# Attention scores, decay and product with v: from 128x128 tiles over two sequences to 64x64 blocks per sequence, in a fused layer on one Trainium2 core

## The chip, the cores and the metric

The kernel runs on one core of a Trainium2 chip. The metric is device time in microseconds of one execution, as a median of repeated runs. The core's engines run side by side and meet only at semaphores: TensorE (PE in the profile; its weight loads are the separate row PEld), VectorE (DVE), ScalarE (ACT), GpSimd (POOL), and SyncE (SP), whose queue issues the DMAs. SBUF and PSUM have 128 partitions. TensorE reads SBUF and writes PSUM, which has eight banks of 128 x 512 float32 here.

## What is computed

x holds 64 sequences of 64 tokens with 512 features. The first half is a gated linear attention with a per-head decay, the second a LoRA-adapted dense layer followed by a ternary feed-forward layer. Cut to what matters:

```python
def _L0_attn_ref(hidden_states, Wq, Wk, Wv, Wb, bb, Wg, Wo, ...):   # H = 16, DK = DV = 128
    q = hidden_states @ Wq; k = hidden_states @ Wk; v = hidden_states @ Wv
    beta = jax.nn.sigmoid(hidden_states @ Wb + bb)
    gate = silu(hidden_states @ Wg)
    q = layernorm(silu(causal_dwconv(q, qconv_w, qconv_b)), qn_w, qn_b)   # per head
    k = layernorm(silu(causal_dwconv(k, kconv_w, kconv_b)), kn_w, kn_b)
    def step(S, inp):
        q_t, k_t, v_t, b_t = inp
        b = b_t[..., None, None]
        S = (1.0 - b) * S + b * (v_t[..., :, None] * k_t[..., None, :])
        o_t = jnp.einsum('bhvk,bhk->bhv', S, q_t)
        return (S, o_t)
    _, os = lax.scan(step, S0, (qs, ks_, vs, bs))
    return (o * gate) @ Wo
x = x + _L0_attn_ref(_L0_cond_ref(x, itok_B_0_7, L0_cond_weights), ...)
x = x + _L0_ffn_ref(_L0_cond2_ref(x, ...), L0_ffn_weight, L0_ffn_bias)
```

The kernel doesn't run the recurrence over tokens. For one head it forms the scores k^T q of every pair of tokens, multiplies them by the decay (the product of 1 - beta between the two tokens, zero where the key comes later or is of another sequence), and multiplies the result with beta * v.

## The kernel before

The 4096 tokens are taken in four groups of 1024. In a group the 16 heads are taken in four sets of four (Fori loop over s), so there are 16 such sets in a run. A set has eight units, n = 0 to 7: a head (n // 2) with one half of the group's tokens (n % 2), which is 512 tokens or eight sequences of 64.

Each engine has its own instruction stream, written out by hand in the loop over n; semaphores tie the streams. On TensorE, iteration n issues: project q(n) (12 float32r matmuls of 512 columns, helper `three`, L959), variance(n-1) (L1031, L1032), project k(n), score(n-2) (L1093), project g(n), attend(n-2) (L1103), centre q and k (L1081, L1082). In iterations 0 and 1 there is no score or attend; the product for v (`values`) is there instead. After iteration 7 comes a tail: output projections (`project_out`, in pieces) with score and attend of units 6 and 7 between them.

The lines around the change:
- score(n), L1093: four matmuls, each of 128 tokens (two sequences) against the same 128, into the bank m0. The trace has two records and two weight loads for each of them.
- scan(n), L703, on VectorE: `tensor_tensor_scan` makes the decay of all 512 columns from `keep` (a row of 1 - beta with zero at each sequence's first token, broadcast to 128 partitions by the DMA at L329) and `ident4`, four identity matrices side by side. Half of each 128x128 tile that results is zero, since it belongs to two different sequences.
- weigh(n), L687, VectorE: decay = m0 * decay, 128 x 512.
- attend(n), L1103: four matmuls of a 128x128 tile of v with the 128x128 tile of decay, into the bank m1.
- gate_out(n), L695 and L697, VectorE: gt = m1 * gt, then a rounded copy to og_hi. POOL makes og_lo from both (L505).
- affine(n), L493, POOL: the last step of the layer norm of q and k, which score(n) waits for.

VectorE's order in iteration n is: three convolution taps of q(n) (L663), scan(n-2), three taps of k(n), weigh(n-2), silu_lo of q and k (L669), newton(n-1) (L644), normalise(n-1) (L653), gate_out(n-2). POOL's is: affine(n-2), scale_centred(n-1) (L486), silu_hi (L499), square_lo(n) (L511), gated_lo(n-2) (L505). In the first group POOL also splits the weights (L450, L452) between these.

score(n) waits for affine(n) and for weigh(n-1), which reads m0. attend(n) waits for weigh(n) and for gate_out(n-1), which reads m1. SP loads `keep` for unit n after scan(n-2) has been done, into one of two halves of the tile, as soon as the waits for weight loads ahead of it in its queue are over.

## Time and profile before

| | us |
|---|---|
| median of 3 runs | 2904.72 |
| lowest, highest | 2903.71, 2907.93 |
| profiled execution, first to last instruction | 2907.7 |

The profiled execution's span is thus 3 us above the median of the runs. In the profile a group of instructions is named by its line, engine, operation and the tiles that it writes and reads; "m" stands for m0 and m1, "gen" for the two variance banks, "r_q", "r_k" and "r_odd" for the normalised q and k of even and odd units. Where a row has a bracket, the engine was idle for that long just before, and the name behind the arrow is what ended the wait ("issue": nothing that the profile shows). Starts and lengths are in us unless marked ns.

### The profile page before, as it was taken

How to read it: one execution, taken by the hardware profiler on the slowest of the kernel's cores; microseconds unless marked ns; L12 is line 12 of the kernel's file. 1: busy time of each engine (PE TensorE's matmuls, PEld its weight loads, DVE VectorE, ACT ScalarE, POOL GpSimd, SP SyncE). 2: the span in 40 equal slices, each digit the busy share in tenths (PEclk: the TensorE clock that was granted, in tenths of full speed). 3: DMA queues.
4: the chain of work that ended last, by engine and by line, in shares of the span. 5: the costliest groups of instructions: out<-in, count | busy, mean ns of one | idle time of the engine just before them, and what ended most of it. 6: DMA issues, size and time to landing. Idle time of an engine off the chain costs nothing.

```text
span 2907.7 us, 40276 instructions
## 1 busy us (share of the span) xinstructions
PE 2585.2 (89%) x12124; PEld 2057.5 (71%) x12136; DVE 1960.1 (67%) x2773; ACT 1561.9 (54%) x2393; POOL 1675.2 (58%) x1450
## 2 busy tenths in 40 slices
PE   4789898898898989999889898989898899998988
PEld 4667676676676777777667776767677677776766
DVE  4484857667658485767666758584865857667685
ACT  2463746456157374746436557483724747565562
POOL 2695968769427374645635637273752646556474
PEclk9999999999999999999999999999999999999999
DMA  6533333333342222222323122222223313222321
GB/s 153 165 117 105 115 108 98 105 98 107 102 135 76 66 90 76 94 65 90 96 94 113 62 97 71 88 83 73 83 94 115 92 63 97 76 83 61 108 88 43
DMA packets 155807, 272.12 MB, mean 94 GB/s; under 512 B 29786, under 2 KB 55898, under 8 KB 155738
## 3 DMA queue, kind: packets, MB, share of 16 engines
q1 hardware_dynamic: 155738, 271.26, 30.0%
q8 instruction: 37, 0.61, 0.1%
q14 instruction: 32, 0.26, 0.0%
HBM read 215.37 MB, written 55.84 MB: 93 GB/s over the span
## 4 chain that ended last, share of the span: by engine, by line
PE 72%; DVE 11%; issue 9%; POOL 4%; ACT 3%; SPq 1%; DMA 0%; POOLq 0%; DVEq 0%; ACTq 0%
PE pj_q L959 22%; PE pj_k L959 14%; PE m L959 10%; PE cen_q L959 4%; PE m L1093 3%; PE m L1103 3%; PE gen L959 3%; PE cen_k L959 3%; PE gen L1031 2%; DVE y_k L663 2%; DVE decay L703 2%; PE gen L1032 2%; DVE acc L710 2%; PE cen_k L1081 1%; POOL og_lo L505 1%
## 5 line engine op out<-in xcount | busy, mean ns | idle before, releaser
L663 DVE SCALAR_TENSOR_TENSOR y_q<-pj_q,conv,y_q 128x504 f32<-128x504 f32 (+2 forms) x384 | 281.5, 733 | 183.3 <-ACT y_q L867 173.4
L959 PE MATMUL pj_k<-ht_hi,wk 128*128 128x512 f32 x1024 | 348.4, 402 | 23.6 <-POOL wk L452 23.6
L511 POOL TENSOR_TENSOR sq_lo_q<-y_q,sq_hi_q 128x512 fp32r<-128x512 f32 x128 | 188.1, 1470 | 304.9 <-ACT y_q L880 304.9
L663 DVE SCALAR_TENSOR_TENSOR y_k<-pj_k,conv,y_k 128x504 f32<-128x504 f32 (+2 forms) x384 | 281.2, 732 | 119.4 <-ACT y_k L867 110.3
L959 PE MATMUL pj_q<-ht_hi,wq 128*128 128x512 f32 x1024 | 343.5, 396 | 12.8 <-DVE acc L710 9.4
L959 PE MATMUL pj_q<-ht_hi,wg 128*128 128x512 f32 x1024 | 346.6, 399 | 1.1 <-POOL wg L452 1.1
L505 POOL TENSOR_TENSOR og_lo<-gt,og_hi 128x512 fp32r<-128x512 f32 x128 | 178.3, 1393 | 149.6 <-DVE og_hi L697 149.6
L959 PEld LDWEIGHTS pj_k<-ht_hi,wk 128*128 128x128 f32 x1024 | 197.8, 193 | 71.7 <-POOL wk L452 27.1
L959 PEld LDWEIGHTS pj_q<-ht_hi,wq 128*128 128x128 f32 x1024 | 194.3, 190 | 64.5 <-DVE acc L710 14.4
L959 PE MATMUL m<-wv,ht_hi 128*128 128x512 f32 x768 | 236.8, 389 | 0.0
L499 POOL TENSOR_SCALAR s_hi_q<-y_q 128x512 fp32r<-128x512 f32 x128 | 79.2, 619 | 259.2 <-ACT y_q L872 259.2
L959 PEld LDWEIGHTS pj_q<-ht_hi,wg 128*128 128x128 f32 x1024 | 192.6, 188 | 40.3 <-issue 1.4
L511 POOL TENSOR_TENSOR sq_lo_k<-y_k,sq_hi_k 128x512 fp32r<-128x512 f32 x128 | 205.2, 1603 | 0.2 <-ACT y_k L880 0.2
L959 PE MATMUL pj_k<-ht_lo,wk 128*128 128x512 f32 x512 | 205.0, 400 | 0.0
L867 ACT ACT_TABLE_LOAD x16 | 20.5, 1283 | 337.9 <-PE pj_q L959 333.4
L959 PE MATMUL pj_q<-ht_lo,wq 128*128 128x512 f32 x512 | 201.0, 393 | 0.0
L959 PE MATMUL pj_q<-ht_lo,wg 128*128 128x512 f32 x512 | 199.8, 390 | 0.0
L679 DVE TENSOR_TENSOR v<-m,beta_tok 128x512 f32<-128x512 f32 x96 | 66.2, 690 | 193.3 <-PE m L959 193.3
L703 DVE TENSOR_TENSOR_SCAN decay<-keep,ident 128x512 f32<-128x512 f32 x128 | 187.2, 1463 | 0.0
L1103 PEld LDWEIGHTS m<-decay,v 128*128 128x128 f32 x1024 | 135.2, 196 | 53.4 <-DVE decay L687 45.5
L1103 PE MATMUL m<-decay,v 128*128 128x128 f32 x1024 | 141.8, 283 | 33.9 <-DVE decay L687 33.4
L959 PEld LDWEIGHTS m<-wv,ht_hi 128*128 128x128 f32 x768 | 144.2, 188 | 30.7
(309 smaller groups left out, 6938.2 us busy)
## 6 DMA issues: line engine op xcount, KB each, us to landing
keep<-keep_rows SPq DMA_DIRECT2D x128, 256.0 KB, 3.4
wo<-parts SPq DMA_DIRECT2D x48, 512.0 KB, 5.9
wq<-parts SPq DMA_DIRECT2D x48, 512.0 KB, 3.6
wk<-parts SPq DMA_DIRECT2D x48, 512.0 KB, 3.6
wg<-parts SPq DMA_DIRECT2D x48, 512.0 KB, 3.6
wv<-parts SPq DMA_DIRECT2D x48, 512.0 KB, 5.8
parts<-wv SPq DMA_DIRECT2D x20, 512.0 KB, 3.4
parts<-wq SPq DMA_DIRECT2D x17, 512.0 KB, 3.0
```

The source lines that it names most:

```text
L499: nc.gpsimd.tensor_scalar(s_hi[x_][:], y[x_][:], 1.0, 0.0, ALU.mult, ALU.add).then_inc(S[f"shi_{x_}"], 1)
L505: nc.gpsimd.tensor_tensor(og_lo[:, n // 2, cols], gt[n % 3][:], og_hi[:, n // 2, cols].bitcast(F32), ALU.subtract).then_inc(S["oglo_done"], 1)
L511: nc.gpsimd.tensor_tensor(sq_lo[x_][:], y[x_][:], sq_hi[x_][:].bitcast(F32), ALU.subtract).then_inc(S[f"sqlo_{x_}"], 1)
L663: V.scalar_tensor_tensor(out=yy[:, :, k:], in0=pp[:, :, :L - k], scalar=conv[:, i, j, 3 - k:4 - k], in1=yy[:, :, k:], op0=ALU.mult, op1=AL ...
L679: V.tensor_tensor(v[:, i, :].rearrange("p (h c) -> p h c", h=SET), v_banks[i][:].rearrange("p (h c) -> p h c", h=SET), bt, ALU.mult).then_ ...
L703: V.tensor_tensor_scan(decay[:], keep[:, n % 2, :], ident4[:].rearrange("p a b -> p (a b)"), 0.0, ALU.mult, ALU.add).then_inc(S["scanned"], 1)
L710: V.tensor_tensor(acc[:, i, :], acc[:, i, :], wo_banks[i % 4][:], ALU.add).then_inc(S["acc_done"], 1)
L959: last = T.matmul(psum, a, b, start=start and n == 0 and m == 0, stop=stop and n == len(pairs) - 1 and m == 2)
L1031: T.matmul(var[x_][:], mean[:], sq_hi[x_][:], start=True, stop=False)
L1032: T.matmul(var[x_][:], mean[:], sq_lo[x_][:], start=False, stop=True).then_inc(S[f"var_{x_}"], 1)
L1093: mm = T.matmul(m0[:, cols], r["k"][n % 2][:, cols], r["q"][n % 2][:, cols], start=True, stop=True)
L1103: mm = T.matmul(m1[:, cols], v[:, HT * (n % 2) + i, (n // 2) * P:(n // 2 + 1) * P], decay[:, cols], start=True, stop=True)
```

## The change

The scores of one sequence need only 64 x 64 values. The change keeps, for a unit, the four even sequences on partitions 0 to 63 and the four odd ones on partitions 64 to 127, each in 256 columns.

- score(n): eight matmuls with 64 columns of weights and 64 moving columns, contraction over 128 partitions. The result of an even sequence goes to partitions 0 to 63 of m0, of an odd one to partitions 64 to 127, at column 64 * (b // 2).
- keep, scan, weigh: all 128 partitions but 256 columns. `keep` is loaded with two DMAs for a unit (one for each half of the partitions), each of 64 partitions x 4 runs of 64 values; the even half has the even sequences' rows. `ident_in` takes the place of `ident4`.
- attend(n): eight matmuls with contraction over 64 partitions (0 to 63 or 64 to 127), 128 columns of weights (v) and 64 moving columns. Even sequences write m1, odd ones m0, 256 columns each.
- gate_out(n): two multiplications of 128 x 256 (m1 for the even, m0 for the odd sequences, with the even or odd 64-column pieces of gt), and the same copy of 512 columns.
- Waits: score(n) now waits for gate_out(n-1) in place of weigh(n-1), as m0 holds a part of attend's result. values(2), which writes m0, waits for the previous set's gate_out.
- Setup: eight copies of 64x64 in place of four of 128x128.

```diff
-        keep = sb("keep", [P, 2, HALF])
+        keep = sb("keep", [P, 2, HPAIRS])
...
-                        sp.dma_start(keep[:, n % 2, :], row.broadcast_to([P, HALF])).then_inc(S[f"keep_in{n % 2}"], 16)
+                        rows = row.rearrange("o (i b t) -> o b i t", b=2, t=L)
+                        for b in range(2):
+                            sp.dma_start(keep[b * L:(b + 1) * L, n % 2, :].rearrange("p (i t) -> p i t", t=L),
+                                         rows[:, b].broadcast_to([L, HT, L])).then_inc(S[f"keep_in{n % 2}"], 16)
...
-                        V.tensor_tensor(decay[:], m0[:], decay[:], ALU.mult).then_inc(S["weighed"], 1)
+                        V.tensor_tensor(decay[:, 0:HPAIRS], m0[:, 0:HPAIRS], decay[:, 0:HPAIRS], ALU.mult
+                                        ).then_inc(S["weighed"], 1)
...
-                        V.tensor_tensor(t[:], m1[:], t[:], ALU.mult).then_inc(S["og_done"], 1)
-                        dve.wait_ge(S["og_done"], of_set("og_done", g, s, UNITS, n + 1))
+                        for b, bank_ in enumerate((m1, m0)):
+                            th = t[:].rearrange("p (i b t) -> p b i t", b=2, t=L)[:, b]
+                            V.tensor_tensor(th, bank_[:, 0:HPAIRS].rearrange("p (i t) -> p i t", t=L), th, ALU.mult
+                                            ).then_inc(S["og_done"], 1)
+                        dve.wait_ge(S["og_done"], of_set("og_done", g, s, 2 * UNITS, 2 * n + 2))
...
-                        V.tensor_tensor_scan(decay[:], keep[:, n % 2, :], ident4[:].rearrange("p a b -> p (a b)"),
+                        V.tensor_tensor_scan(decay[:, 0:HPAIRS], keep[:, n % 2, :], ident_in[:].rearrange("p a b -> p (a b)"),
...
-                        pe.wait_ge(S["weighed"], of_set("weighed", g, s, UNITS, n))
+                        pe.wait_ge(S["og_done"], of_set("og_done", g, s, 2 * UNITS, 2 * n))
...
-                        for i in range(HT):
-                            cols = slice(i * P, (i + 1) * P)
-                            mm = T.matmul(m0[:, cols], r["k"][n % 2][:, cols], r["q"][n % 2][:, cols], start=True, stop=True)
+                        for b in range(HROWS):
+                            cols, at = slice(b * L, (b + 1) * L), L * (b % 2)
+                            mm = T.matmul(m0[at:at + L, b // 2 * L:(b // 2 + 1) * L], r["k"][n % 2][:, cols],
+                                          r["q"][n % 2][:, cols], start=True, stop=True)
...
-                        pe.wait_ge(S["og_done"], of_set("og_done", g, s, UNITS, n))
...
-                        for i in range(HT):
-                            cols = slice(i * P, (i + 1) * P)
-                            mm = T.matmul(m1[:, cols], v[:, HT * (n % 2) + i, (n // 2) * P:(n // 2 + 1) * P],
-                                          decay[:, cols], start=True, stop=True)
+                        for b in range(HROWS):
+                            at, cols = L * (b % 2), slice(b // 2 * L, (b // 2 + 1) * L)
+                            mm = T.matmul((m1, m0)[b % 2][:, cols],
+                                          v[at:at + L, HT * (n % 2) + b // 2, (n // 2) * P:(n // 2 + 1) * P],
+                                          decay[at:at + L, cols], start=True, stop=True)
```

TensorE's stream at the score of an odd unit, before (m is m0 here; each row is an instruction of the program, x3 three more like it):

```order
L959 MATMUL pj_k<-ht_hi,wk 128x512
L1093 MATMUL m<-r_odd 128x128 [waits weighed,aff_k,aff_q]
L1093 MATMUL m<-r_odd 128x128 x3
L1054 REGISTER_ALU
L959 MATMUL pj_q<-ht_hi,wg 128x512 [waits tap_q]
```

and in the changed kernel:

```order
L969 MATMUL pj_k<-ht_hi,wk 128x512
L1098 REGISTER_ALU [waits aff_k,aff_q]
L1103 MATMUL m<-r_odd 64x64 [waits og_done]
L1103 MATMUL m<-r_odd 64x64 x7
L1064 REGISTER_ALU
L969 MATMUL pj_q<-ht_hi,wg 128x512 [waits tap_q]
```

The score stands at the same place between project k and project g; it is eight matmuls in place of four, and waits for og_done in place of weighed. VectorE's stream at gate_out, before:

```order
L653 SCALAR_TENSOR_TENSOR r_odd<-t_k,c_k 128x512 [waits rc_k,t2_k]
L695 TENSOR_TENSOR gt<-m,gt 128x512 [waits gated,pv]
L697 CAST og_hi<-gt 128x512 [waits og_done]
L663 SCALAR_TENSOR_TENSOR y_q<-pj_q,conv,y_q 128x8x63 [waits tap0_q]
L662 REGISTER_ALU
```

and in the changed kernel:

```order
L659 SCALAR_TENSOR_TENSOR r_odd<-t_k,c_k 128x512 [waits rc_k,t2_k]
L704 TENSOR_TENSOR gt<-m,gt 128x4x64 [waits gated,pv]
L704 TENSOR_TENSOR gt<-m,gt 128x4x64
L706 ISA
L707 CAST og_hi<-gt 128x512 [waits og_done]
L669 SCALAR_TENSOR_TENSOR y_q<-pj_q,conv,y_q 128x8x63 [waits tap0_q]
```

One more multiplication stands ahead of the copy; the rest of the stream keeps its order.

## Rows read from the trace of the kernel before

**Rows 1.** The page: busy time of each engine, and the chain's shares.
```profile
PE 2585.2 (89%) x12124; PEld 2057.5 (71%) x12136; DVE 1960.1 (67%) x2773; ACT 1561.9 (54%) x2393; POOL 1675.2 (58%) x1450
...
PE 72%; DVE 11%; issue 9%; POOL 4%; ACT 3%; SPq 1%; DMA 0%; POOLq 0%; DVEq 0%; ACTq 0%
```

**Rows 2.** Timeline of one middle iteration: start, length, engine, line, operation, tiles, count.
```profile
1062.28 0.68 DVE L695 TENSOR_TENSOR gt<-m,gt 128x512 f32<-128x512 f32 x1
...
1063.58 0.47 PE L1031 MATMUL gen<-sq_hi_k,mean 128*128 128x512 f32 x1 [0.94 <-issue]
...
1063.85 1.29 POOL L505 TENSOR_TENSOR og_lo<-gt,og_hi 128x512 fp32r<-128x512 f32 x1 [0.36 <-DVE og_hi L697]
...
1065.13 0.77 POOL L493 TENSOR_SCALAR r_odd<-r_odd,ln_q 128x512 f32<-128x512 f32 x1
...
1065.87 1.26 DVE L703 TENSOR_TENSOR_SCAN decay<-keep,ident 128x512 f32<-128x512 f32 x1
1065.88 1.74 POOL L493 TENSOR_SCALAR r_odd<-r_odd,ln_k 128x512 f32<-128x512 f32 x1
...
1067.73 1.13 PE L1093 MATMUL m<-r_odd 128*128 128x128 f32 x8 [0.68 <-issue]
...
1068.61 0.48 PE L959 MATMUL pj_q<-ht_hi,wg 128*128 128x512 f32 x1
...
1068.93 0.39 PE L959 MATMUL pj_q<-ht_lo,wg 128*128 128x512 f32 x1
...
1071.45 1.05 PE L1103 MATMUL m<-decay,v 128*128 128x128 f32 x8
...
1072.26 0.48 PE L1081 MATMUL cen_q<-s_hi_q,center 128*128 128x512 f32 x1
...
1072.80 0.69 DVE L644 SCALAR_TENSOR_TENSOR t_q<-gen,t_q 128x512 f32<-128x512 f32 x1 [0.15 <-ACT t_q L858]
...
1081.77 1.13 PE L1093 MATMUL m<-r_q,r_k 128*128 128x128 f32 x8 [0.67 <-issue]
```

**Rows 3.** Timeline, the same set's iterations 2 and 3.
```profile
1023.27 2.31 DVE L703 TENSOR_TENSOR_SCAN decay<-keep,ident 128x512 f32<-128x512 f32 x1
...
1028.40 1.82 PE L1103 MATMUL m<-decay,v 128*128 128x128 f32 x8 [1.86 <-DVE decay L687]
...
1037.86 2.36 DVE L703 TENSOR_TENSOR_SCAN decay<-keep,ident 128x512 f32<-128x512 f32 x1
```

**Rows 4.** Waits of the whole run: total us, times, longest us.
```profile
PE m L1103 <- DVE decay L687: 33.4, 21, 1.9
```

**Rows 5.** Timeline, the same set's tail.
```profile
1113.59 1.22 DVE L703 TENSOR_TENSOR_SCAN decay<-keep,ident 128x512 f32<-128x512 f32 x1
...
1113.76 2.11 POOL L505 TENSOR_TENSOR og_lo<-gt,og_hi 128x512 fp32r<-128x512 f32 x1 [1.72 <-DVE og_hi L697]
...
1115.92 0.74 PE L959 MATMUL cen_q<-wo,og_hi 128*128 128x512 f32 x2 [1.39 <-POOL og_lo L505]
```

**Rows 6.** Groups by line and shape: busy us, mean ns of one, idle before.
```profile
L703 DVE TENSOR_TENSOR_SCAN decay<-keep,ident 128x512 f32<-128x512 f32 x128 | 187.2, 1463 | 0.0
...
L663 DVE SCALAR_TENSOR_TENSOR y_q<-pj_q,conv,y_q 128x504 f32<-128x504 f32 x128 | 94.6, 739 | 174.1 <-ACT y_q L867 173.4
...
L663 DVE SCALAR_TENSOR_TENSOR y_q<-pj_q,conv,y_q 128x488 f32<-128x488 f32 x128 | 93.0, 726 | 4.6
...
L695 DVE TENSOR_TENSOR gt<-m,gt 128x512 f32<-128x512 f32 x128 | 87.2, 682 | 105.4 <-PE m L1103 105.4
```

**Rows 7.** The shortest float32 matmuls of the trace, as a group (columns as rows 6).
```profile
L1019 PE MATMUL m<-ident,y_k 16*128 16x16 f32 x16 | 1.6, 206 | 2.1 <-ACT y_k L842 2.1
```

**Rows 8.** Timeline, four of these matmuls in a row.
```profile
60.30 0.39 PE L1019 MATMUL m<-ident,y_k 16*128 16x16 f32 x4 [0.51 <-ACT y_k L842]
```

**Rows 9.** Timeline of SP's queue: the load of keep for unit 7.
```profile
1100.61 0.33 SPq L329 DMA_DIRECT2D keep<-keep_rows  x1
```

**Rows 10.** The page's DMA issues: count, KB each, us from issue to landing.
```profile
keep<-keep_rows SPq DMA_DIRECT2D x128, 256.0 KB, 3.4
```

More of the change, by code:

```diff
@@ L50, in adaln_attn_ffn @@
     PAIRS = TILES // 2
+    HPAIRS = HALF // 2
     SMALL = 10
@@ L91, in adaln_attn_ffn @@
         ident_bf = sb("ident_bf", [P, P], BF16)
-        ident4 = sb("ident4", [P, HT, P])
+        ident_in = sb("ident_in", [P, HT, L])
         center = sb("center", [P, P], F32R)
@@ L135, in adaln_attn_ffn @@
         SETUP_LOADS = 1 + KC + 4 + 4 + 1 + 2
-        SETUP_DVE = 33
+        SETUP_DVE = 37
         pj = {"q": bank("pj_q"), "k": bank("pj_k")}
@@ L580, in _ @@
             for t in range(HT):
-                step(V.tensor_copy(ident4[:, t, :], ident[:]))
+                for b in range(2):
+                    half = slice(b * L, (b + 1) * L)
+                    step(V.tensor_copy(ident_in[half, t, :], ident[half, half]))
             dve.wait_ge(S["wb_in"], 16)
@@ L694, in gate_out @@
                         dve.wait_ge(S["gated"], of_set("gated", g, s, UNITS, n + 1))
-                        V.tensor_tensor(t[:], m1[:], t[:], ALU.mult).then_inc(S["og_done"], 1)
-                        dve.wait_ge(S["og_done"], of_set("og_done", g, s, UNITS, n + 1))
+                        for b, bank_ in enumerate((m1, m0)):
[3 more added lines that the diff above has]
+                        dve.wait_ge(S["og_done"], of_set("og_done", g, s, 2 * UNITS, 2 * n + 2))
                         V.tensor_copy(hi, t[:]).then_inc(S["oghi_done"], 1)
                     def scan(n):
-                        dve.wait_ge(S[f"keep_in{n % 2}"], of_set(f"keep_in{n % 2}", g, s, UNITS // 2 * 16, 16 * (n // 2 + 1)))
+                        dve.wait_ge(S[f"keep_in{n % 2}"], of_set(f"keep_in{n % 2}", g, s, UNITS // 2 * 32, 32 * (n // 2 + 1)))
                         dve.wait_ge(S["pv"], of_set("pv", g, s, UNITS, n))
-                        V.tensor_tensor_scan(decay[:], keep[:, n % 2, :], ident4[:].rearrange("p a b -> p (a b)"),
+                        V.tensor_tensor_scan(decay[:, 0:HPAIRS], keep[:, n % 2, :], ident_in[:].rearrange("p a b -> p (a b)"),
                                              0.0, ALU.mult, ALU.add).then_inc(S["scanned"], 1)
@@ L965, in _ @@
             pe.wait_ge(S["setup_in"], 16 * SETUP_LOADS)
-            pe.wait_ge(S["setup_dve"], 7)
+            pe.wait_ge(S["setup_dve"], 11)
             for k in range(KC):
@@ L980, in _ @@
             mm.then_inc(S["setup_pe"], 1)
-            pe.wait_ge(S["setup_dve"], 29)
+            pe.wait_ge(S["setup_dve"], 33)
             for t in range(KC):
@@ L1065, in values @@
                             pe.wait_ge(S["beta_tok_done"], of_group("beta_tok_done", g, 1, 1))
-                            pe.wait_ge(S["weighed"], of_set("weighed", g, s, UNITS, 0))
+                            pe.wait_ge(S["og_done"], of_set("og_done", g, s, 2 * UNITS, 0))
                         elif i == 3:
-                            pe.wait_ge(S["og_done"], of_set("og_done", g, s, UNITS, 0))
+                            pe.wait_ge(S["og_done"], of_set("og_done", g, s, 2 * UNITS, 0))
                         else:
```

## Prediction

> **What bounds the kernel now.** I read the page's busy times and its chain first, then the timeline of a middle iteration, of the start of a set and of its tail, then the waits, the groups by shape, and the DMA lines.
>
> TensorE is busy for 89% of the span and carries 72% of the chain, with 9% of "issue" in it [rows 1]. That reads like a TensorE bound with small gaps; the gaps are what to look at. In a middle iteration TensorE stops twice: 0.94 us before the variance of k, and 0.68 us before the score [rows 2]. The second has no releaser in the profile, but POOL's affine of k runs from 1065.88 for 1.74 us and so ends at 1067.62, 0.11 us before the score's start at 1067.73: the score waits for POOL. From one score to the next it is 1081.77 - 1067.73 = 14.04 us. The loop that closes in this time is: score, project g, ACT's squares of r, VectorE's newton (which waits only 0.15 us, for ACT), normalise and gate_out, POOL's og_lo (which waits 0.36 us for VectorE), affine of q, affine of k, and again the score. TensorE has 0.94 + 0.68 = 1.6 us of slack in it, VectorE and POOL next to none.
>
> Two more places stop TensorE. In iteration 2 of the set the first attend waits 1.86 us for weigh [rows 3]; over the run this wait stands 21 times with 33.4 us, the longest 1.9 [rows 4]: once in each of the 16 sets (16 x 1.86 = 29.8) and a few shorter ones in iteration 3. Behind it is VectorE, whose scan takes 2.31 us there and 2.36 in iteration 3 [rows 3] against 1.26 in a middle iteration [rows 2]. And in the tail an output projection waits 1.39 us for og_lo [rows 5].
>
> **The change, part by part.** Sums are made against the profiled execution, 2907.7 us, which stands 3 us above the median of the runs.
>
> *The scan*, half as many columns. Its mean is 1463 ns, and the shortest kind 1.22 us [rows 5, 6]. By columns it halves to about 0.65, with a fixed part that stays to 0.75 or so. What counts is where it stands. In a middle iteration it has idle time behind it, but it runs beside POOL's affine of k, and that takes 1.74 us where the affine of q just before takes 0.77 [rows 2]. The excess of 0.97 us comes with a scan of 1.26 at the same start; the tail shows it again (og_lo of 2.11 us beside a scan of 1.22, against 1.29 elsewhere, an excess of 0.82) [rows 2, 5]. I take the excess to shrink with the scan: -0.45 us (between 0, if it isn't the scan's doing, and -0.6). In iterations 2 and 3 the scan lies on VectorE's path to weigh: 2.31 halves to 1.15.
>
> *weigh*, half the columns. *gate_out*, two halves in place of one whole. A 512-column product from PSUM takes 682 ns [rows 6]. The half-size one lies between 341 ns (all by column) and 474: three taps of other widths give a slope, 739 - 726 = 13 ns for 16 columns, 0.81 ns a column, so 682 - 256 x 0.81 = 474 [rows 6]. I take 0.42. weigh then gains 0.26, and gate_out costs 2 x 0.42 - 0.68 = +0.16 us (0 to 0.27). gate_out is on the closing loop: og_lo waits for it.
>
> *Middle iterations (n = 4 to 7), VectorE and POOL alone*: -0.45 + 0.16 = -0.3 us on the loop above. A second loop (variance, project k, taps, silu, silu_lo, newton) is only 0.15 us behind it by VectorE's wait [rows 2] and gains nothing but part of weigh. I take -0.25 an iteration, 4 x -0.25 = -1.0 us a set.
>
> *Iterations 2 and 3*: weigh(0) comes 1.15 + 0.26 = 1.4 us earlier; the 1.86 us wait covers that fully, so -1.4. In iteration 3 the scan again gives up to 1.2, but the taps of k can't start before TensorE's project k and ACT's first tap, so only half of it counts: -0.6. Together -2.0 us a set.
>
> *Tail*: og_lo -0.4, gate_out +0.16: -0.25 us a set.
>
> VectorE and POOL together give -(1.0 + 2.0 + 0.25) = -3.25 us a set, x 16 = -52 us.
>
> *Score and attend on TensorE*: this is the unknown. Now eight records of 128 columns take 0.88 us from the score to project g (1067.73 to 1068.61) and 0.81 from attend to centre (1071.45 to 1072.26) [rows 2], 0.11 and 0.10 a record. The change makes sixteen of each, with half the moving columns. The trace has no record of 64 columns. The nearest are the transposes with 16 moving columns and 128 columns of weights: four take 0.39 us with the last's own 0.206, so (0.39 - 0.206) / 3 = 0.061 us a record [rows 7, 8]. That is the price if a record with few columns is bound by its weight load and issue. Upper end: 0.11 a record as now, because the weights of attend are still 128 columns wide: 16 x 0.11 = 1.76, +0.9 us. Lower end: the two halves of the array work at once and a pair costs what one record of half the columns costs: 16 x 0.028 = 0.44, -0.45 us. I take 0.061, the row it is nearest to in size: 16 x 0.061 = 0.98, so +0.10 for the score and +0.17 for attend.
>
> *Change of shape in the array*: after the score the first matmul of project g takes 0.32 us to the next (1068.61 to 1068.93), where such matmuls follow at 0.23 [rows 2]. A switch back thus costs 0.09 already. Going from a whole array to halves may add the same once more around each of the two: +0.1 for the pair (0 to 0.4).
>
> The Trainium skill ("TensorEngine Tiling (Array Packing)", Key Properties) says that a change of the tiling mode drains TensorE, and that distinct tiles load weights and multiply in parallel. No row here shows a switch between tilings of the kind the change brings; the first sentence would put the cost of the switches to the upper end, the second that of the records to the lower.
>
> So a unit costs TensorE 0.10 + 0.17 + 0.1 = +0.37 us. Of that the two units in the tail count whole, as TensorE runs there without other slack. The six before them lie partly under waits (TensorE's 1.6 us of slack in the middle, 0.46 left of the 1.86 at the start), but the score itself is on the closing loop: I count half. 2 + 6 / 2 = 5 units a set: 5 x 0.37 = 1.85 us, x 16 = +30 us.
>
> *Costs of nothing.* The score's new wait for gate_out(n-1): it starts at 1062.28 and would end by 1063.2, the score comes at 1067.73 [rows 2]; 4.5 us of cover, and project g and all behind it would queue if that were gone. The wait of values(2) has longer cover (two projections and a v product lie between). The keep loads: twice the DMAs, runs of 256 bytes, half the bytes. The latest of a set is issued at 1100.61 and used by the scan at 1113.59 [rows 5, 9]; 13 us of cover for something that lands in 3.4 [rows 10]. Behind it on SP's queue stand only the next set's loads. Setup: four more small copies that TensorE's first transposes wait for, under 1 us in all.
>
> **Sum**: 2907.7 - 52 + 30 = 2885.7 in the profiled execution, 2883 as a median.
>
> **The rivals.**
>
> *A. Records near 0.06 us, as above.* Between a pair cost of +0.15 and +0.6 us a unit: -52 + 80 x 0.15 = -40 to -52 + 48 = -4 us, so 2865 to 2901. Chance 0.45.
>
> *B. The weight loads rule (slower).* The place is attend: its weights are as wide as before and there are twice as many, so sixteen records at 0.11. With the score at 0.061 and the switches: 0.10 + 0.9 + 0.1 = +1.1 us a unit, x 80 = +88, less 52 = +36: 2941. If the score's records too stay at 0.11 (a load that can't run beside the matmul before it): +1.9 a unit, +100 us, 3005. It decides for slower at 52 / 80 = 0.65 us a unit. For it: nothing in the trace shows two weight loads at once. Against it: the 16-column row has the same 128 columns of weights and comes at 0.061. The Trainium skill ("TensorE: Matmul & The Clock Gate", The mechanism) says that a weight load overlaps a matmul in flight only when the row group differs. The score's halves share their rows, and by that its loads would stand bare, as in the second form of this rival; attend's would be hidden. Chance 0.30, of which 0.06 for both.
>
> *C. The halves run at once.* -0.3 to -0.45 us for each of score and attend, against +0.1 for switches: -0.6 us a unit. Where TensorE isn't the bound that gives less: the tail's 2 units whole, of the six others a third: 4 x -0.6 x 16 = -38, with -52: -90, so 2815. Between A and C (-60) lies 2845. For it: the two halves have their own partitions in and out. Chance 0.20.
>
> *D. The excess on POOL's affine isn't the scan's*, and with gate_out longer the middle doesn't gain: +0.1 an iteration in place of -0.25, 4 x 0.35 x 16 = +22 on A: 2905, no change. Chance 0.05.
>
> **How the numbers follow.** The forecast is A's middle, 2883. The range takes in C down to 2830 and the first form of B up to 2950, and leaves out the last part of C and the second form of B, with the tails of the others about 0.2. A measurement here can tell 0.2%, 5.8 us. Faster: A but for its last part (0.40), all of C (0.20), some of D (0.01) make 0.61. Same: A's end, part of B's low end and D, 0.09. Slower: 0.30.
>
> **What would show it.** Right: the score's wait in a middle iteration below 0.5 us, POOL's affine of k near 1.3, scans of 0.7, the first attend's wait of 1.86 down to about 0.5, sixteen score records within 1.0 us, middle iterations of about 13.9 us. Wrong: attend of 1.7 us or more from its start to the centring (B), of 0.6 or less (C), an affine of k still at 1.7 beside a scan of 0.7 (D), or keep landing after the scan asks for it.

## The result, and the profile after

The changed kernel takes 2879.9 us (median; 2878.1 to 2887.6), the kernel before 2904.8. The ratio is 0.9916, with a 95% interval of 0.9902 to 0.993: faster by 0.8%. The profiled execution spans 2876.0 us against 2907.7, so there are 31.7 us to account for.

The page of the kernel after, busy times, the DMA queue that carries instructions, and the chain's shares (as [rows 1]):

```profile
PE 2600.1 (90%) x14172; PEld 2007.4 (70%) x14184; DVE 1863.6 (65%) x2905; ACT 1571.0 (55%) x2393; POOL 1604.2 (56%) x1450
...
q8 instruction: 149, 2.44, 0.3%
...
PE 59%; POOL 13%; issue 13%; DVE 10%; ACT 4%; SPq 1%; DMA 0%; POOLq 0%; DVEq 0%; ACTq 0%
```

VectorE lost 97 us of work and POOL, whose work was not touched, 71 us. TensorE has 2048 more matmul records (two for each of 1024 more matmuls of the program), and the chain, 72% TensorE before, now lies 59% on it.

Timeline of a middle iteration after (start, length, engine, line, operation, tiles, count; as [rows 2]). L704 is gate_out, L509 og_lo, L497 the affine, L713 the scan, L1103 score, L1113 attend:

```profile
1063.19 0.74 DVE L704 TENSOR_TENSOR gt<-m,gt 128x256 f32<-128x256 f32 x2
...
1066.05 0.78 POOL L497 TENSOR_SCALAR r_odd<-r_odd,ln_q 128x512 f32<-128x512 f32 x1
1066.79 0.70 DVE L713 TENSOR_TENSOR_SCAN decay<-keep,ident_in 128x256 f32<-128x256 f32 x1
1066.81 1.25 POOL L497 TENSOR_SCALAR r_odd<-r_odd,ln_k 128x512 f32<-128x512 f32 x1
...
1068.30 0.69 PE L1103 MATMUL m<-r_odd 128*64 128x64 f32 x16 [0.33 <-POOL r_odd L497]
1068.92 0.50 PE L969 MATMUL pj_q<-ht_hi,wg 128*128 128x512 f32 x1
...
1071.86 1.11 PE L1113 MATMUL m<-decay,v 64*128 64x64 f32 x16
1072.90 0.50 PE L1091 MATMUL cen_q<-s_hi_q,center 128*128 128x512 f32 x1
...
1082.02 0.69 PE L1103 MATMUL m<-r_q,r_k 128*64 128x64 f32 x16 [0.37 <-POOL r_k L497]
```

The scan went from 1.26 to 0.70 us, and POOL's affine of k beside it from 1.74 to 1.25. The score waits 0.33 us in place of 0.68 and comes every 13.72 us (1082.02 - 1068.30) in place of 14.04. The score's sixteen records last 0.62 us to the next matmul, where eight took 0.88; attend's take 1.04 where eight took 0.81.

The start of a set and its tail (as [rows 3] and [rows 5]): the first attend's wait is 1.14 us for 1.86, and og_lo takes 1.60 us for 2.11.

```profile
1026.21 1.77 DVE L713 TENSOR_TENSOR_SCAN decay<-keep,ident_in 128x256 f32<-128x256 f32 x1
1030.53 1.11 PE L1113 MATMUL m<-decay,v 64*128 64x64 f32 x16 [1.14 <-DVE decay L693]
...
1113.65 1.60 POOL L509 TENSOR_TENSOR og_lo<-gt,og_hi 128x512 fp32r<-128x512 f32 x1 [2.25 <-DVE og_hi L707]
...
1115.30 0.73 PE L969 MATMUL cen_q<-wo,og_hi 128*128 128x512 f32 x2 [0.73 <-POOL og_lo L509]
```

**The gain isn't even.** The starts of the attends cut the span into pieces. I use two: the mean time from one set to the next in group 3 (in these two kernels groups 1 and 2 give the same within 0.3), and the time from the first attend of group 0 to the first of group 1. Group 0 has four sets as well, but POOL also splits the weights there.

| us | before | after | difference |
|---|---|---|---|
| start to first attend | 128.89 | 126.54 | -2.4 |
| group 0, to group 1's first attend | 742.9 | 750.2 | +7.3 |
| from there to the end (12 sets) | 2035.9 | 1999.3 | -36.6 |
| one set in group 3 | 156.74 | 153.87 | -2.9 |

Groups 1 to 3 gained twice what I forecast (1.4 us a set), and group 0 lost. The two misses nearly cancel. The experiments ask for the cause of each.

### The profile page after: what moved, and what is told of

It is laid out like the page before. It is cut to its first block, busy times and chain, and to the rows that moved or that the text cites. A ratio compares the mean times of both kernels' runs of the same rounds, so it can differ in the third digit from the quotient of the medians.

```text
span 2876.0 us, 45128 instructions
## 1 busy us (share of the span) xinstructions
PE 2600.1 (90%) x14172; PEld 2007.4 (70%) x14184; DVE 1863.6 (65%) x2905; ACT 1571.0 (55%) x2393; POOL 1604.2 (56%) x1450
## 3 DMA queue, kind: packets, MB, share of 16 engines
q8 instruction: 149, 2.44, 0.3%
## 4 chain that ended last, share of the span: by engine, by line
PE 59%; POOL 13%; issue 13%; DVE 10%; ACT 4%; SPq 1%; DMA 0%; POOLq 0%; DVEq 0%; ACTq 0%
PE pj_q L969 17%; PE m L969 10%; PE pj_k L969 9%; PE cen_q L969 5%; POOL sq_lo_k L515 4%; PE m L1113 3%; PE gen L969 3%; DVE y_k L669 3%; PE cen_k L969 3%; POOL r_odd L497 2%; PE m L1103 2%; POOL sq_lo_q L515 2%; DVE acc L720 1%; ACT y_q L890 1%; POOL og_lo L509 1%
## 5 line engine op out<-in xcount | busy, mean ns | idle before, releaser
L515 POOL TENSOR_TENSOR sq_lo_q<-y_q,sq_hi_q 128x512 fp32r<-128x512 f32 x128 | 191.7, 1498 | 279.5 <-ACT y_q L890 279.5
L509 POOL TENSOR_TENSOR og_lo<-gt,og_hi 128x512 fp32r<-128x512 f32 x128 | 170.1, 1329 | 174.3 <-DVE og_hi L707 174.3
L515 POOL TENSOR_TENSOR sq_lo_k<-y_k,sq_hi_k 128x512 fp32r<-128x512 f32 x128 | 206.7, 1615 | 0.3 <-ACT y_k L890 0.3
L704 DVE TENSOR_TENSOR gt<-m,gt 128x256 f32<-128x256 f32 x256 | 95.3, 411 | 124.9 <-PE m L1113 124.9
L1113 PEld LDWEIGHTS m<-decay,v 64*128 64x128 f32 x2048 | 124.2, 187 | 64.6 <-DVE decay L693 37.1
```

Of the source, the lines that this page charges most:

```text
L509: nc.gpsimd.tensor_tensor(og_lo[:, n // 2, cols], gt[n % 3][:], og_hi[:, n // 2, cols].bitcast(F32), ALU.subtract).then_inc(S["oglo_done"], 1)
L515: nc.gpsimd.tensor_tensor(sq_lo[x_][:], y[x_][:], sq_hi[x_][:].bitcast(F32), ALU.subtract).then_inc(S[f"sqlo_{x_}"], 1)
L704: V.tensor_tensor(th, bank_[:, 0:HPAIRS].rearrange("p (i t) -> p i t", t=L), th, ALU.mult).then_inc(S["og_done"], 1)
L1113: mm = T.matmul((m1, m0)[b % 2][:, cols], v[at:at + L, HT * (n % 2) + b // 2, (n // 2) * P:(n // 2 + 1) * P], decay[at:at + L, cols], star ...
```

## Experiments

The same two pieces for every kernel that ran (in the order in which they are told), with the ratio to the kernel before on the same chip:

| kernel | us | ratio, 95% interval | one set, group 3 | group 0 |
|---|---|---|---|---|
| before | 2904.8 | | 156.74 | 742.9 |
| after | 2879.9 | 0.9916 (0.9902 to 0.993) | 153.87 | 750.2 |
| b_half | 2865.4 | 0.986 (0.9844 to 0.9877) | 153.39 | 742.3 |
| b_scan | 2868.3 | 0.9862 (0.9845 to 0.9878) | 153.71 | 740.8 |
| a_full | 2928.1 | 1.008 (1.006 to 1.0101) | 156.89 | 755.1 |
| b_split | 2997.3 | 1.0311 (1.0288 to 1.0334) | 162.88 | 761.5 |
| a_grouped | 2913.4 | 1.0024 (1.0015 to 1.0034) | 157.49 | 740.4 |
| a_pad | 2885.3 | 0.992 (0.9903 to 0.9936) | 154.13 | 753.3 |
| a_mix | 2873.3 | 0.9879 (0.9857 to 0.9901) | 153.88 | 740.7 |
| a_wait | 2904.2 | 0.9986 (0.9976 to 0.9995) | 153.84 | 771.2 |
| a_ksplit | 2866.4 | 0.986 (0.9842 to 0.9877) | 153.68 | 735.0 |
| a_best | 2864.0 | 0.9853 (0.9837 to 0.9869) | 153.90 | 732.4 |
| a_again | 2880.4 | 0.9912 (0.9897 to 0.9927) | 153.86 | 752.3 |
| a_grouped2 | 2914.4 | 1.0025 (1.0015 to 1.0035) | 157.35 | 742.7 |

### b_half and b_scan: VectorE's part of the change alone

```diff
-V.tensor_tensor_scan(decay[:], keep[:, n % 2, :], ident4[:]...,
+V.tensor_tensor_scan(decay[:, 0:256], keep[:, n % 2, 0:256], ident4[:]...[:, 0:256],
-V.tensor_tensor(decay[:], m0[:], decay[:], ALU.mult)
+V.tensor_tensor(decay[:, 0:256], m0[:, 0:256], decay[:, 0:256], ALU.mult)   # b_half alone
```

> The kernel before with VectorE's part of the change alone: scan and weigh run over the first 256 columns, TensorE's matmuls stay 128x128 (the second half of the decay stays zero, so half of the product is left out). Theory of the prediction (the scan's excess over the q-q scale-and-shift and the shorter weigh reach TensorE in the middle iterations, the second iteration's attend wait falls in full): -0.41 us in four middle iterations, -2.0 in iterations 2 and 3, -0.25 in the tail, x16 sets = about -62, 2843 us; aff_k near 1.3 us, scan near 0.7, attend's wait of iteration 2 near 1.1. Rival (the halves count at every place of VectorE at once): -0.9 us in every iteration, 2790. Rival (group 0 gives it back by itself, because POOL and VectorE meet at a worse moment there): groups 1 to 3 gain, from the first attend of group 0 to that of group 1 the time grows from 743 us, total near 2860.

> The kernel before with the scan alone over 256 columns; weigh stays 512 wide and multiplies by the constant identity in place of the decay, so the decay is left out of the output. The both-halves kernel b_half measured 2865.4 us, 40 below before. By the prediction's terms (scan -0.45 and weigh -0.26 a middle iteration, and in iterations 2 and 3 mostly the scan) the scan alone gives about two thirds: -27, 2879 us, middle iterations 13.8 to 13.85 us. Rival (the middle iteration already stands at another bound after the scan, since b_half, after and a_full all show 13.7 to 13.8): nearly all of it in groups 1 to 3, -34, 2871. Rival (weigh carries it): 2893.

b_half leaves out the second half of each product, and b_scan the decay. b_half saves 3.35 us a set in group 3 and 0.6 us in all of group 0. Its forecast was 3.9 a set (62 / 16), and so 15 in group 0: the prediction's 3.25 had the longer gate_out in it, which b_half doesn't have. b_scan saves 3.03 of the 3.35: the scan is nine tenths of it, where two thirds were expected, and weigh's shorter half is worth 0.3 us a set. So the halves gave most of what was expected of them in twelve sets and nothing in four. The last rival of b_half, group 0 giving it back by itself, is what came.

### a_full: TensorE's part alone

```diff
-V.tensor_tensor_scan(decay[:, 0:HPAIRS], ...
+V.tensor_tensor_scan(decay[:], ...            # second half: zeros
-V.tensor_tensor(decay[:, 0:HPAIRS], m0[:, 0:HPAIRS], decay[:, 0:HPAIRS], ALU.mult
+V.tensor_tensor(decay[:], m0[:], decay[:], ALU.mult
```

> The kernel after with scan and weigh over 512 columns again (the second 256 columns carry zeros that nobody reads), so TensorE's 64-wide tiles, the split gate and the smaller keep loads stand alone. Theory of the prediction: TensorE +0.37 us a unit x5 x16 = +30 and the split gate +0.16 x4 x16 = +10, so 2945 us; by what the trace after shows (+0.09 for the stage score, +0.23 for attend in the tail, a score that is shorter beside it) +0.22 a unit, 2933. Rival (tiles cost nothing net, the score records at 0.031 us pay for attend's): 2905 to 2915. In each case TensorE waits 2.3 to 2.6 us for its own instructions at the end of sets 0 to 2 of group 0, if the longer set loop is what causes it.

The tiles and the split gate cost 22 us over before; 2945 and 2933 were expected, and 2905 to 2915 by the rival. In group 0 they cost 12 us, and in group 3 0.15 us a set. Over all twelve sets of groups 1 to 3 it is 0.47 (2041.5 us for 2035.9). In the four sets of group 1 and the first of group 2 the granted clock falls to 0.50, its lower level of 1.2 GHz, for 2 us and more behind the first attend's wait of 1.95 us. These sets take 157.5 to 157.9 us, and those of group 3, where it stays at 1.00 there, 156.9. Counted the other way, after against b_half, the tiles cost 0.48 us a set and 8 us in group 0. Both say that the term forecast at 1.85 us a set is at most 0.5, and that the larger share is group 0's. There about 5 us of it sit at the three ends of sets, where the TensorE loop goes back to its start. The rows are a_full's, then after's (timelines of TensorE):

```profile
246.10 0.77 PE L971 MATMUL pj_q<-ht_hi,wq 128*128 128x512 f32 x1 [2.81 <-issue]
```
```profile
244.82 0.47 PE L969 MATMUL pj_q<-ht_hi,wq 128*128 128x512 f32 x1 [2.65 <-issue]
```

Before, the same matmul waits 0.78 us for VectorE's acc.

### a_grouped and b_split: what a record costs

```diff
-for b in range(HROWS):                  # a_grouped, in score and attend
+for b in (0, 2, 4, 6, 1, 3, 5, 7):
```
```diff
-mm = T.matmul(m0[:, cols], r["k"][n % 2][:, cols], r["q"][n % 2][:, cols], ...)   # b_split, x4
+mm = T.matmul(m0[:, half], r["k"][n % 2][:, cols], r["q"][n % 2][:, half], ...)   # x8, attend alike
```

> The kernel after with the four even sequences first and then the four odd ones in score and attend, the rest untouched. Theory 1 (the two halves of the array work at once, because even and odd alternate): score records go from 0.031 to about 0.06 us, attend's from 0.055 to about 0.09 or more; +0.45 and +0.5 us a unit, +75 us, 2955. Theory 2 (a record costs what it costs, alternation buys nothing): same within 5 us of 2880.

> The kernel before with each matmul of score and attend over 128 columns issued as two over 64 columns, with the same 128x128 weights: as many TensorE instructions in the set loop as after, no tiles of 64, no other change. Theory (the set loop's length is what makes TensorE wait 2.5 us for instructions at the ends of sets 0 to 2 of group 0): that wait shows here too, with more instruction packets on the DMA queues between 230 and 600 us. Rival (the 64 KB keep loads or the tile modes cause it): no such wait. The stages: if a 64-column record costs its columns, 16 records take as long as 8 before (about 0.45 us) and the time is 2905 to 2915 with the wait; if a weight load of 128 rows bounds it (0.06 us a record), +0.45 us a stage, two stages, 80 units: +70, 2980.

First a_grouped's two stages in a middle iteration with the matmul behind each, then b_split's attend:

```profile
1067.50 1.60 PE L1113 MATMUL m<-decay,v 64*128 64x64 f32 x16
1069.03 0.50 PE L1091 MATMUL cen_q<-s_hi_q,center 128*128 128x512 f32 x1
...
1077.67 0.97 PE L1103 MATMUL m<-r_q,r_k 128*64 128x64 f32 x16
1078.57 0.50 PE L969 MATMUL pj_q<-ht_hi,wg 128*128 128x512 f32 x1
```
```profile
1067.19 1.89 PE L1103 MATMUL m<-decay,v 128*128 128x64 f32 x16
1068.89 0.48 PE L1081 MATMUL cen_q<-s_hi_q,center 128*128 128x512 f32 x1
```

The stage is counted to the start of the next matmul. Inside it the records' own start times in the trace give the step from one to the next (medians over the run's 128 stages):

| us | score: stage | step | attend: stage | step |
|---|---|---|---|---|
| before, 128x128 weights, 128 columns | 0.88 | 0.112 | 0.81 | 0.112 |
| b_split, 128x128 weights, 64 columns | 1.70 | 0.112 | 1.70 | 0.112 |
| a_grouped, tiles of one half in a row | 0.90 | 0.058 | 1.53 | 0.112 |
| after, the halves in turn | 0.62 | 0.058 a pair | 1.04 | 0.112 a pair |

b_split says that halving the moving columns alone gives nothing: a record with whole weights comes every 0.112 us at 64 columns as at 128, so what bounds it isn't the columns (0.06 was expected). a_grouped says that a half-width weight tile (128x64, the score) halves the price and a half-height one (64x128, attend) doesn't. Then after says what the turns bring: the two records of a pair start 0.01 us apart, and the pair costs what one record of a half costs. So the two halves of the array do work beside each other. That is worth 0.28 us in the score and 0.49 in attend, from the order of eight matmuls alone, 33 us over the run. (a_grouped's expectation had 75 for it: the stages did grow as it said, but most of that lay under waits.)

By the step, after's stages should last 0.46 and 0.90 us, eight pairs each. The rest is at their edges: 0.15 us in the score and 0.14 in attend. Before, the stages are 0.01 and 0.09 shorter than their eight steps, and b_split's 0.09 shorter than their sixteen. And attend starts 0.32 us behind the matmul ahead of it, in after and a_grouped alike, for 0.23 in before and b_split. So a unit pays 0.16 + 0.23 + 0.09 = 0.48 us for going into the tiles and out of them, and gets 8 x 0.054 = 0.43 back in the score.

The Trainium skill ("TensorE: Matmul & The Clock Gate", The mechanism) says that a weight load overlaps a running matmul only when the row group differs. The score's tiles all use the same 128 rows, and a pair of them costs no more than one record in a row; and with whole weights the step stays at 0.112 us for 64 moving columns as for 128, which it couldn't if the load had to wait for the matmul to end. In this case that sentence doesn't hold.

b_split was expected to show the 2.5 us wait at the ends of sets, and neither kernel does, though both have as many TensorE instructions in the loop as after, and the same 149 instruction packets in place of 37. That speaks against length as a sufficient cause.

### a_pad, a_again and a_grouped2: the wait for instructions

```diff
+for k in range(8 * KC):                 # a_pad, once, in TensorE's setup
+    T.transpose(m0[:, k % KC * P:...], a_src[:, k % KC * P:...], ident[:])
```

> The kernel after with 32 more transposes of 128x128 once in TensorE's setup, into a buffer that is overwritten: no work changes in the loops, only where their instructions lie in TensorE's program. The change's longer loop brings instruction packets in every set, yet b_split and a_grouped, whose loops are as long, show no wait at the set ends and after and a_full show 2.3 to 2.8 us. Theory 1 (where the loop lies against the packets' borders decides): the waits of TensorE at the ends of sets 0 to 2 of group 0 change, to 0 to 3 us each, or show up elsewhere; 2873 to 2890 us. Theory 2 (TensorE runs through the end of the set too fast for the supply: shorter stages): they stay at 2.3 to 2.6 us and the time is 2880 to 2884.

> The kernel after once more, unchanged. If TensorE's wait for instructions at the ends of sets 0 to 2 belongs to the program, it shows again, 3 times 2.3 to 2.8 us (as in after, a_full, a_pad, a_wait); if it belongs to one execution, it is shorter or missing. Time 2880, and group 0 from first attend to first attend 750 us.

> a_grouped once more, unchanged. Its group 0 is instruction for instruction that of a_mix, which showed waits for instructions of 5.9 us in 3 times where a_grouped showed none. If these waits vary from one execution to the next, this one may show either, and the time stays 2913 within its spread; if the code of groups 1 to 3 decides (its order differs from a_mix's), none again.

The wait of the set's first matmul in group 0, at the ends of sets 0, 1 and 2:

| kernel | us | releaser |
|---|---|---|
| before, b_half | 0.78, 0.78, 0.78 | acc |
| b_split | 0.97, 0.78, 0.78 | acc |
| a_grouped | 1.09, 1.53, 1.00 | acc |
| a_grouped2 | 1.68, 1.59, 1.94 | acc, acc, issue |
| a_best (below) | 1.51, 1.94, 1.51 | acc, issue, acc |
| a_mix (below) | 2.19, 1.98, 1.74 | issue |
| after | 2.65, 2.41, 2.30 | issue |
| a_again | 2.48, 2.89, 2.24 | issue |
| a_full | 2.81, 2.62, 2.36 | issue |
| a_pad | 2.91, 2.75, 2.07 | issue |
| a_ksplit (below) | 2.94, 2.23, 2.62 | issue |
| a_wait (below) | 3.02, 2.37, 2.20 | issue |

The same kernel gives much the same wait again. Moving the loop within the program (a_pad) doesn't shorten it, but it changes the packets, 68 for 149:

```profile
q8 instruction: 68, 1.11, 0.2%
```

By the packets' start times in the trace, after has nine from one first attend to the next in every group. a_pad has nine a set in group 0 and none in half the sets of groups 1 to 3, which take as long as after's (2001.1 us for 1999.3): packets there cost nothing.

The wait goes with the moment at which one packet lands. In all 31 waits of the table over 0.78 us, a packet has landed 1.75 to 1.89 us before the matmul starts, whatever the stages take. In groups 1 to 3 of the kernels with the long loop it lands 2.1 to 2.9 us before it (a_pad has none there), and the matmul waits 0.78 us for acc each time. Before and b_half have no packet within 3 us of the turn. b_split, which has the long loop without the tiles and the new keep loads, has the packets: the loop brings them. The longer the score and attend take in such a kernel, the shorter the wait: 2.1 to 3.0 us with the halves in turn, 1.0 to 2.2 grouped, 0.8 to 1.0 with whole weights. All this fits instructions which arrive at a pace of their own. The trace doesn't say which engine a packet is for, so that this one is TensorE's is inferred from the times. Why it comes earlier against the matmul in groups 1 to 3, with a loop that differs by a few waits, isn't settled.

The Trainium skill ("Runtime: NRT & Kernel Launch", Instruction fetch mechanics) says that a taken branch to a target no longer held forces a fetch before the engine goes on. The packets agree with its block of 16 KiB (2.44 MB / 149), and a wait at the turn of the loop fits; by it alone groups 1 to 3 of after, which have packets at the same place, should wait as well, and they don't.

### a_mix and a_wait: the rest of group 0

```diff
-for b in range(HROWS):                                                          # a_mix
+for b in ((0, 2, 4, 6, 1, 3, 5, 7) if first else range(HROWS)):
```
```diff
 if first:
     split_next(*mid[n])
+    pool.wait_ge(S["n_k"], of_set("n_k", g, s, UNITS, n))                       # a_wait
 square_lo("q", n)
```

> The kernel after with even sequences first and odd ones after them (as in a_grouped) in group 0 alone, alternating in groups 1 to 3. a_grouped went from the first attend of group 0 to that of group 1 in 740.3 us, after in 750.2, before in 742.9, though a_grouped's stages are 0.3 to 0.7 us longer. Theory (group 0's loss is one of phase and of instruction supply, groups 1 to 3 don't depend on it): -10, 2870 us, no wait of TensorE for instructions at the set ends. Rival (a_grouped's gain in group 0 hung on something else, or the start of group 0 differs): 2880.

> The kernel after, with one more wait on POOL in group 0: the low part of the squares of iteration n starts only when VectorE has normalised q and k of iteration n-1. Theory (in group 0 POOL's subtraction and VectorE's normalisation start together in iterations 4 and 6, each normalisation takes 1.8 us instead of 0.7, and the delay reaches the split of the k weights): the 1.8 us rows go from group 0, attend to attend across iterations 3-4 and 5-6 falls from 19.2 to 20 us towards 18.3, 8 times, about -8: 2872 us. Rival (POOL is itself the bound of these iterations, and the wait only pushes its splits back): they grow, 2885 to 2895.

The timeline after in set 1 of group 0, iteration 4, shows what I suspected. L515 is POOL's low part of the squares, L659 VectorE's normalise, L454 and L456 POOL's split of the k weights:

```profile
316.53 1.30 POOL L515 TENSOR_TENSOR sq_lo_q<-y_q,sq_hi_q 128x512 fp32r<-128x512 f32 x1
316.56 1.82 DVE L659 SCALAR_TENSOR_TENSOR r_q<-t_q,c_q 128x512 f32<-128x512 f32 x1
317.78 1.75 POOL L515 TENSOR_TENSOR sq_lo_k<-y_k,sq_hi_k 128x512 fp32r<-128x512 f32 x1
318.30 1.77 DVE L659 SCALAR_TENSOR_TENSOR r_k<-t_k,c_k 128x512 f32<-128x512 f32 x1
...
321.28 1.26 POOL L509 TENSOR_TENSOR og_lo<-gt,og_hi 128x512 fp32r<-128x512 f32 x1 [1.75 <-DVE og_hi L707]
322.51 0.62 POOL L454 TENSOR_SCALAR wk<-raw 128x512 fp32r<-128x512 f32 x1
323.21 1.26 POOL L456 TENSOR_TENSOR wk<-raw,wk 128x512 fp32r<-128x512 f32 x1
...
324.53 0.79 PE L969 MATMUL pj_k<-ht_hi,wk 128*128 128x512 f32 x1 [3.95 <-POOL wk L456]
```

Both normalises take 1.8 us beside POOL's subtractions, where one alone takes 0.68. All 107 slow ones of after have a tensor_tensor of POOL beside them that started first; but 85 others overlap one as well and take 0.68. In group 0, 10 of 32 normalises of q do so after, 2 before, 8 in b_half, none in a_grouped and a_mix.

a_mix gains what a_grouped had shown: group 0 in 740.7 us in place of 750.2, and groups 1 to 3 stay. Slower matmuls thus made the kernel faster by 7 us (the intervals of the two ratios lie side by side, 0.9901 and 0.9902; the 9.5 us of group 0 are clearer). Its waits at the ends of sets, which were expected to go, shrank by 1.5 us in all. But that alone doesn't say whether the collisions or the waits are its cause. a_wait removes every slow normalise in group 0, and the steps around iterations 4 and 6 do fall, from 19.3 us on average to 18.7. Yet POOL, held back in every iteration, comes 8.3 us later to the first attend, 5.6 us at each end of a set and 0.9 to 2.5 in the tail, and the kernel is 24 us slower, beyond what the rival had (2885 to 2895). What the wait buys is 0.6 us, 8 times; the collision isn't the main cause.

### a_ksplit and a_best: POOL's queue in group 0

What is left in the rows above is the order on POOL: og_lo waits 1.75 us for VectorE and runs 1.26, and only then comes the split that TensorE stands for.

```diff
-if 1 < n < UNITS - 1:
-    gated_lo(n - 2)
 if first and n in late:
     split_next(*late[n])
+if 1 < n < UNITS - 1:
+    gated_lo(n - 2)
```

> The kernel after, with POOL's split of the k weights in iterations 3 and 5 of group 0 put ahead of og_lo instead of behind it. In the trace after og_lo waits 1.75 us for VectorE's og_hi and then runs 1.26 us before that split (1.9 us), while TensorE stands 3.95 us before pj_k; 8 such waits of TensorE sum to 30.5 us (23.6 before, 31.2 in b_half). Theory (this place, POOL's queue behind VectorE, is what gave back the halved scan in group 0): the waits fall by about 3 us each to a sum of 6 to 10 us, group 0 from first attend to first attend falls from 750 to about 728, total 2858 us. Rival (POOL's time is owed anyway, og_lo and the scale-and-shift behind it are then late, or TensorE's instruction waits grow): 2870 to 2880.

> a_ksplit and a_mix together: the k split ahead of og_lo, and even sequences first in group 0 alone. a_mix measured 2873.3 with a pj_k wait of 19.8 us in 8 times. If the two gains add: -15 on 2873, 2858. If they are the same gain (both shorten the wait for the k split) the longer stages of the grouped order cost 0.6 us a unit in group 0, 32 units, about +10 against a_ksplit: 2865 to 2870.

The waits of TensorE for the k weights, after and then a_ksplit (us in total, times, longest us), and the same place in a_ksplit's timeline:

```profile
PE pj_k L969 <- POOL wk L456: 30.5, 8, 4.0
```
```profile
PE pj_k L969 <- POOL wk L456: 11.2, 8, 1.4
PE pj_q L969 <- POOL wg L456: 9.1, 8, 1.1
```
```profile
315.44 1.07 POOL L454 TENSOR_SCALAR wk<-raw 128x512 fp32r<-128x512 f32 x1
316.59 1.26 POOL L456 TENSOR_TENSOR wk<-raw,wk 128x512 fp32r<-128x512 f32 x1
317.91 0.50 PE L969 MATMUL pj_k<-ht_hi,wk 128*128 128x512 f32 x1 [1.41 <-POOL wk L456]
```

The wait fell by 19 us and a new one, for the weights of g, took 9 back: POOL's time is owed in part, as the rival had it. The whole is -14 us against after on the same chip (2866.4 and 2880.4); theory had said 2858. It comes with the slow normalises of q unchanged (10 of 32), so the order of POOL's queue, not the collision, is what costs most in group 0. That the halved scan by itself gave nothing there (b_half) comes by the same wait: it grew from 23.6 us to 31.1. a_best, with the grouped order in group 0 as well, gives 2864.0. The two can't be told apart (their intervals overlap), and both beat the kernel before by 1.4% and the kernel after by 0.5%.

## Why the prediction was right, and where it wasn't

2883.0 was forecast and 2879.9 came. The sign and the account of the gain on VectorE and POOL hold, but for group 0; the account of TensorE's part doesn't, and the closeness is partly luck.

- **The halves on VectorE and POOL, -52 us.** Measured alone (b_half), -40, where the same terms without the longer gate_out made -62. In groups 1 to 3 the size was nearly right (3.9 a set forecast, 3.35 to 3.43 measured) though its parts were not. In after the four steps between middle iterations gave -1.4 us, where I had -1.0 without TensorE's share; the first step gave -0.5, and the attend's wait fell by 0.7 of the 1.4 us forecast, since the shorter scan still takes 1.77 us beside POOL in iteration 2 (1.15 forecast); and the tail and the turn of the set gave -0.9 (12.39 + 61.72 to 12.00 + 61.19), where I had -0.25. The affine's excess fell from 0.97 to 0.47 us (1.25 - 0.78), as the step on the scan said, and that rules out D. What failed is the step "x 16": it carried the rows of one set in group 1 over to group 0, where POOL also splits weights and TensorE waits 23.6 us for them already in the trace of before (and 31.1 in b_half). There an earlier VectorE only meets a later POOL. This row was in the waits of before, and I didn't use it:

```profile
PE pj_k L959 <- POOL wk L452: 23.6, 8, 3.9
```

- **Sixteen records in place of eight, +30 us with the switches.** Measured +0.15 to +0.5 us a set in groups 1 to 3, 2 to 6 us in all, for a forecast of 1.85 a set. The term was near for attend and 0.36 us too high for the score (0.62 us and not 0.98), and the mechanism was another one. Attend came at 1.04 for 0.98 forecast, but for another reason than the one given. The 0.061 of [rows 7, 8] isn't the price of such a record, though the score's 0.058 lies near it: attend's records have B's price, 0.112 us for weights of 128 columns. And C's premise holds in full: a pair of the two halves costs one record. B's price for a stage without turns shows in b_split and in a_grouped's attend. For the score C had 16 x 0.028 = 0.44 us, and its eight pairs take 0.46. Neither rival's time came, since attend's price and the edges of the stages take back what the pairs give. In a middle iteration the tiles cost nothing (13.7 us in b_half as in after), the tail and the turn of the set pay (11.82 + 60.93 in b_half, 12.00 + 61.19 after).
- **Switches, +0.1 us a unit.** Mis-sized. The first matmul behind the score takes 0.33 us to the next (1068.92 to 1069.25), as before (0.32), so the place that I read shows nothing. But the edges of the two stages and the step into attend cost 0.48 us a unit more than before, over my upper end of 0.4. The records gave 0.43 back, where I had them at +0.27. The unit's +0.05 us in place of +0.37 is the difference of two terms that were both wrong.
- **Costs of nothing.** The score's wait for gate_out never shows, and keep lands in 2.8 us with no wait of the scan. Right. What I left out is the loop's length: 128 more matmul records a set and as many weight loads brought 7.4 us of waits for instructions in group 0, 5.0 more than the same matmul waits before (3 x 0.78). There is no step for it in the prediction; the queue for instructions, with its 37 packets, stands on the page of the kernel before.
- **What would show it.** Score's wait 0.33 (under 0.5), affine 1.25 (1.3), scans 0.70 (0.7), the score's stage 0.62 (within 1.0), iterations of 13.72 (13.9): all came. The half product of gate_out takes 0.41 (0.42). The first attend's wait is 1.14, not 0.5.

So the sum, in the profiled executions: -44.9 us from VectorE and POOL alone (b_half), and from there to after +4.6 in groups 1 to 3, +7.9 in group 0 (5.0 of it the waits for instructions) and +0.8 ahead of the first attend, make the 31.7 measured. The medians moved by 25. The forecast had -22, from other parts, and a VectorE term that was too large was met by a TensorE term that was too large: that is the luck in it.

## What to carry over

Split a many-stage loop by its phases before multiplying a gain by the number of rounds: a phase in which another engine has extra work can take the whole gain, and the trace of before shows that engine waited for. Small matmuls on tiles of the array should alternate between halves; in these runs the price of a record is set by its weights and its neighbour, not by its moving columns, and each stage of tiles pays at its edges. After a change that lengthens a loop, look at the queue that carries instructions and at the first matmul behind the loop's turn.

## What the runs showed that I had not expected

- A float32 record with 128x128 weights comes every 0.112 us with 64 moving columns as with 128. With 128x64 weights it is 0.058, with 64x128 0.112, and two records on different halves of the array cost together what one costs.
- The order of eight matmuls on two halves of the array is worth 0.28 us (score) and 0.49 us (attend) a stage.
- VectorE's normalise takes 1.8 us in place of 0.68 beside a subtraction on POOL that started first, though not beside each, and POOL's own instruction 1.3 to 1.75 us; a 256-column scan takes 0.70 or 1.77 us, by what POOL does.
- With 256 more TensorE instructions in a loop, instruction packets go from 37 to 149, and the engine may wait 2 to 3 us at the loop's turn, less if its stages are slower; the matmul there starts 1.75 to 1.89 us behind the landing of a packet.
- Before, the granted clock was 0.73 on the mean from 1030 to 1034 us, so part of it at the lower level (1.2 GHz), just behind the first attend's wait of 1.86 us, and that attend lasted 1.7 to 2.0 us in 6 of 16 sets; after, with a wait of 1.14 us, none does. The sets that begin so take 0.1 to 0.5 us longer than the others of their group, by estimate 2 us in all at most. The last set of group 0 has the lower level too (0.50 from 634 to 638 us), and its first step takes 16.6 us in place of 14.8.
